# A graph layer's first stage: two node chunks beside each edge group, and an earlier release of a PSUM tile

## The reference, cut to what matters

```python
xn = layernorm(x)                                    # 20000 x 256
h = silu(edge_attr_8 @ fc_w1 / sqrt(8))              # radial network, first product
w = (h @ fc_w2 / sqrt(64)).reshape(-1, 5, 64)        # second product: five weights per channel
s, v = xn[:, :64][src], xn[:, 64:].reshape(-1, 64, 3)[src]
m0 = (w[:, 0] * s + w[:, 3] * dot(v, sh1) / sqrt(3)) / sqrt(2)
m1 = (w[:, 1] * s * sh1 + w[:, 2] * v + w[:, 4] * cross(v, sh1) / sqrt(2)) / sqrt(3)
x = x + xn + concat(segment_sum(m0, dst) @ lin_w0, segment_sum(m1, dst) @ lin_w1) / (16 * 8)
x = x + experts(layernorm(x))                        # later stages, not touched
```

## Time and profile before

| | us |
|---|---|
| median of three runs | 1472.23 |
| the profiled execution's own time | 1472.45 |
| its span, first to last instruction | 1470.6 |
| start of the next stage's loads (SP, line 354) | 386.23 |

### The profile page before, as it was taken

One profiled execution on the slowest core, in us unless ns is written; L12 is line 12 of the kernel. 1 busy time (PEld: TensorE's weight loads), 2 busy tenths in 40 slices (PEclk: granted clock), 3 DMA queues, 4 the chain that ended last, 5 costly groups with the idle time before them and its releaser, 6 DMA issues.

```text
span 1470.6 us, 26642 instructions
## 1 busy us (share of the span) xinstructions
PE 1217.7 (83%) x7872; PEld 1077.1 (73%) x7872; DVE 1007.6 (69%) x2132; ACT 930.6 (63%) x2048; POOL 1029.5 (70%) x975
## 2 busy tenths in 40 slices
PE   2335598898499433999999999999999999999993
PEld 0222365555355222999999999999999999999993
DVE  7889969997399795655756755755755575556653
ACT  4788967875266400666766766666766676657662
POOL 6886787875488402776777766777776777678785
PEclk9966788889799775999999999999999999999997
DMA  9999845543666302233433432243522343233333
GB/s 328 295 338 321 265 83 72 76 66 47 143 215 216 116 10 71 66 82 45 107 47 51 106 49 43 48 104 47 113 45 46 45 108 51 46 47 52 53 52 43
DMA packets 131626, 152.98 MB, mean 104 GB/s; under 512 B 17034, under 2 KB 118474, under 8 KB 131422
## 3 DMA queue, kind: packets, MB, share of 16 engines
q0 software_dynamic: 51456, 64.07, 27.0%
q1 hardware_dynamic: 58446, 66.59, 13.9%
q10 hardware_dynamic: 21648, 21.45, 4.2%
HBM read 98.79 MB, written 53.28 MB: 103 GB/s over the span
## 4 chain that ended last, share of the span: by engine, by line
PE 54%; issue 3%; POOL 2%; ACT 1%; DMA 1%; DVE 0%; ACTq 0%; POOLq 0%; DVEq 0%
PE f_ps_y L1523 26%; PE f_ps_h L1511 25%; PE f_ps_x L1501 2%; POOL out L1402 1%; POOL xg L1384 1%; POOL sg L1388 0%; DMA sg<-stat_rows,idx_row 0%; ACT y_all L1461 0%; ACT h_all L1451 0%; ACT h_hi L1450 0%; ACT f_xn L1435 0%; DMA out<-clean,put_now 0%; DMA sg<-stat_rows,idx_now 0%; DVE clean L1588 0%; DVE x_lo L1556 0%
## 5 line engine op out<-in xcount | busy, mean ns | idle before, releaser
L1450 ACT ACTIVATE h_hi<-f_ps_h,c_b 128x384 fp32r<-128x384 f32 (+1 forms) x416 | 236.8, 569 | 262.7 <-PE f_ps_h L1511 262.7
L1561 DVE TENSOR_TENSOR h_lo<-h_all,h_hi 128x768 fp32r<-128x768 f32 (+1 forms) x208 | 184.4, 887 | 256.9 <-ACT h_all L1451 256.3
L1523 PE MATMUL f_ps_y<-w_hi,h_hi 128*128 128x256 f32 x1136 | 325.4, 286 | 0.0
L1523 PE MATMUL f_ps_y<-w_lo,h_hi 128*128 128x256 f32 x1136 | 320.4, 282 | 0.0
L1523 PE MATMUL f_ps_y<-w_hi,h_lo 128*128 128x256 f32 x1136 | 320.2, 282 | 0.0
L1402 POOL DMA_INDIRECT out<-clean,put_now x159 | 262.0, 1648 | 56.7 <-issue 49.4
L1384 POOL DMA_INDIRECT xg<-out,idx_now x159 | 192.7, 1212 | 129.6 <-issue 119.4
L1511 PE MATMUL f_ps_h<-x_hi,w_hi 128*128 128x384 f32 (+1 forms) x832 | 272.3, 327 | 8.0 <-issue 3.5
L1511 PE MATMUL f_ps_h<-x_lo,w_hi 128*128 128x384 f32 (+1 forms) x832 | 269.8, 324 | 0.0
L1511 PE MATMUL f_ps_h<-x_hi,w_lo 128*128 128x384 f32 (+1 forms) x832 | 269.5, 324 | 0.0
L1451 ACT ACTIVATE h_all<-f_ps_h,c_b 128x384 f32<-128x384 f32 (+1 forms) x416 | 237.7, 571 | 0.0
(11 more groups left out here) (211 smaller groups left out, 2290.2 us busy)
## 6 DMA issues: line engine op xcount, KB each, us to landing
shared<-out SPq DMA_DIRECT2D x40, 512.0 KB, 4.0
w_raw<-in_w SPq DMA_DIRECT2D x16, 1024.0 KB, 5.4
xin<-in_x SPq DMA_DIRECT2D x24, 512.0 KB, 7.2
out<-xin ACTq DMA_DIRECT2D x24, 512.0 KB, 6.4
shared<-in_x SPq DMA_DIRECT2D x16, 512.0 KB, 6.7
out<-shared ACTq DMA_DIRECT2D x16, 512.0 KB, 6.1
dst_row<-in_dst SPq DMA_DIRECT2D x20, 256.0 KB, 3.9
xg<-out,idx_now POOLq DMA_INDIRECT x159
```

What stands on the lines that cost most here:

```text
L1450: nc.scalar.activation(h_hi[:, f, :n * P], ps_h[:, f % SLOTS, :n * P], ACT.Relu, bias=b1[:, e, f:f + 1])
L1523: ins = nc.tensor.matmul(ps_y[:, i], x[:, f, i * P:(i + 1) * P], weights[s][:, w], start=i != 1 and f == 0 and n == 0, stop=f == KF - 1 an ...
L1561: tt(h_lo[:, pair, :n * P], h_all[j % 2][:, :, :n * P], h_hi[:, pair, :n * P].bitcast(F32), ALU.subtract).then_inc(h_lo_ready, 1)
```

## The change

`STEPS` becomes 10. DVE takes two node chunks in each of steps 0 to 7, one of them inside `messages`. ACT adds two chunks for each group, in loops 1 to 9. The buffers of edge statistics go from four to eight (`AHEAD`), and DVE's statistics of edge groups run ahead: groups 3 to 9 in steps 0 to 3 (two a step), then group n in step n - 6, so that group 19 is done in step 13. POOL issues two gathers, one batch of node statistics and two of edge statistics in each round, and its last own node batch is number 6. Its gathers 14 to 19 now follow scatters 5, 6 and 7. The reciprocal square roots of edge groups 10 to 19 follow scatters 3 to 12. SP sends the embeddings and receivers of a group with each second chunk.

In `messages` the last reader of ps_w is brought forward by one instruction and raises a semaphore of its own, `w_taken`. PE's second product waits for that instead of `msg_ready`. PE's first product is issued before the aggregate. ACT copies the aggregate between the two halves of `rows_by_direction`, and the update behind the second.

```diff
@@ -136,13 +136,14 @@
     RING = 6
-    STEPS = 5
+    STEPS = 10
+    AHEAD = 8
     SLOTS = 14
...
     MAGIC = 0x5F3759DF
-    BY_POOL = 8
-    assert NC == 4 * STEPS
+    BY_POOL = 7
+    assert NC == 2 * STEPS
     with ExitStack() as ctx:
...
@@ -201,10 +202,10 @@
         edge_stats = [sb(f"edge_stats{h}", [P, GT, 6]) for h in range(2)]
-        edge_mv = [sb(f"edge_mv{h}", [P, GT, 2]) for h in range(4)]
+        edge_mv = [sb(f"edge_mv{h}", [P, GT, 2]) for h in range(AHEAD)]
         edge_var = sb("edge_var", [P, GT])
-        edge_rstd = [sb(f"edge_rstd{h}", [P, GT]) for h in range(4)]
-        edge_shift = [sb(f"edge_shift{h}", [P, GT]) for h in range(4)]
+        edge_rstd = [sb(f"edge_rstd{h}", [P, GT]) for h in range(AHEAD)]
+        edge_shift = [sb(f"edge_shift{h}", [P, GT]) for h in range(AHEAD)]
         y = [sb(f"y{h}", [P, GT, 4, D]) for h in range(2)]
...
@@ -262,6 +263,7 @@
         msg_ready = sem("msg_ready")
+        w_taken = sem("w_taken")
         row_ready = sem("row_ready")
...
@@ -320,31 +322,26 @@
             for c in range(NC):
-                for a in range(2):
-                    if 1 <= c and c + RING - 1 < NC:
+                if c:
+                    for a in range(2):
                         sp.wait_ge(x1_out[(c - 1) % RING][a], 16 * ((c - 1) // RING + 1))
-                        load_rows(c + RING - 1, a)
-                if 1 <= c and c + RING - 1 < NC:
+                        if c + RING - 1 < NC:
+                            load_rows(c + RING - 1, a)
                     sp.sem_inc(stored, 1)
...
                     sp.dma_start(chunks_needed[:], io["chunks"].rearrange("g o -> o g")).then_inc(chunks_known, 16)
-                if c % 4 == 1:
-                    next_embedding(c // 4)
-                    if c > 4:
-                        next_receivers(c // 4 - 1)
-            for c in range(NC - RING, NC):
-                for a in range(2):
-                    sp.wait_ge(x1_out[c % RING][a], 16 * (c // RING + 1))
-                sp.sem_inc(stored, 1)
-                if c == NC - RING + 1:
-                    next_receivers(STEPS - 1)
-                if c == NC - RING + 3:
-                    next_embedding(STEPS)
-            next_receivers(STEPS)
-            for g in range(STEPS + 1, EG):
+                if c % 2:
+                    next_embedding(c // 2)
+                    if c > 2:
+                        next_receivers(c // 2 - 1)
+            for a in range(2):
+                sp.wait_ge(x1_out[(NC - 1) % RING][a], 16 * ((NC - 1) // RING + 1))
+            sp.sem_inc(stored, 1)
+            next_receivers(STEPS - 1)
+            for g in range(STEPS, EG):
                 next_embedding(g)
...
@@ -370,12 +367,12 @@
             def edge_scales(g):
-                h = g % 4
+                h = g % AHEAD
                 pool.wait_ge(edge_mv_ready, g + 1)
...
                     pool.wait_ge(edge_rstd_ready, g)
-                if g >= 4:
-                    pool.wait_ge(y_first, g - 3)
+                if g >= AHEAD:
+                    pool.wait_ge(y_first, g - AHEAD + 1)
                 chain.link(nc.gpsimd.tensor_scalar(edge_var[:], edge_mv[h][:, :, 1], EPS, None, ALU.add))
...
@@ -422,20 +419,21 @@
             for n in range(3, BY_POOL):
+                gather(2 * n - 1)
+                gather(2 * n)
                 node_scales(n)
-                for g in (2 * n - 1, 2 * n):
-                    if g < SLOTS:
-                        gather(g)
-                if n % 2:
-                    edge_scales(n // 2 + 2)
+                edge_scales(2 * n - 3)
+                if 2 * n - 2 < STEPS:
+                    edge_scales(2 * n - 2)
+            gather(2 * BY_POOL - 1)
             pool.wait_ge(chunks_known, 16)
...
                 scatter(g)
-                if STEPS <= g + 4 < EG - 1:
-                    edge_scales(g + 5)
-                if 1 <= g < 4:
-                    gather(SLOTS + 2 * g - 2)
-                    gather(SLOTS + 2 * g - 1)
+                if STEPS <= g + 7 < EG:
+                    edge_scales(g + 7)
+                if 5 <= g < 8:
+                    gather(SLOTS + 2 * (g - 5))
+                    gather(SLOTS + 2 * (g - 5) + 1)
             pool.wait_ge(scattered, 64 * (EG + 1))
@@ -454,8 +452,8 @@
                     ins = nc.scalar.activation(y[g % 2][:, t, 0, :], rows[g][:, t, :], ACT.Identity,
-                                               bias=edge_shift[g % 4][:, t:t + 1],
-                                               scale=edge_rstd[g % 4][:, t:t + 1])
+                                               bias=edge_shift[g % AHEAD][:, t:t + 1],
+                                               scale=edge_rstd[g % AHEAD][:, t:t + 1])
                 ins.then_inc(y_first, 1)
@@ -510,31 +508,30 @@
             rows_by_direction(0, (2, 3))
-            add_own_rows(2)
             radial_hidden(1)
...
             rows_by_direction(1, range(GT))
-            add_own_rows(3)
             for g in range(1, STEPS):
-                c = 4 * g
-                add_own_rows(c)
+                add_own_rows(2 * g)
+                radial_hidden(g + 1)
+                if g + 1 == STEPS:
+                    add_own_rows(2 * g + 1)
+                    store_rows(NC - 1, 1)
+                next_rows(g + 1)
+                rows_by_direction(g + 1, (0, 1))
                 take_agg(g - 1)
-                radial_hidden(g + 1)
-                next_rows(g + 1)
-                add_own_rows(c + 1)
-                rows_by_direction(g + 1, (0, 1))
+                if g + 1 < STEPS:
+                    add_own_rows(2 * g + 1)
+                rows_by_direction(g + 1, (2, 3))
                 take_upd(g - 1)
-                add_own_rows(c + 2)
-                rows_by_direction(g + 1, (2, 3))
-                add_own_rows(c + 3)
-            store_rows(NC - 1, 1)
             for g in range(STEPS, EG + 1):
                 if g + 1 < EG:
+                    radial_hidden(g + 1)
                     next_rows(g + 1)
-                    rows_by_direction(g + 1, range(GT))
+                    rows_by_direction(g + 1, (0, 1))
                 take_agg(g - 1)
                 if g + 1 < EG:
-                    radial_hidden(g + 1)
+                    rows_by_direction(g + 1, (2, 3))
                 take_upd(g - 1)
@@ -548,7 +545,7 @@
                 if g:
-                    pe.wait_ge(msg_ready, g)
+                    pe.wait_ge(w_taken, g)
                 for t in range(GT):
...
@@ -583,9 +580,9 @@
                     radial_second(g + 1)
-                aggregate(g)
                 if g + 2 < EG:
                     radial_first(g + 2)
+                aggregate(g)
                 transform(g)
@@ -655,10 +652,10 @@
                 chain.link(ins)
-                if g >= 4:
-                    v.wait_ge(coef_ready, g - 3)
+                if g >= AHEAD:
+                    v.wait_ge(coef_ready, g - AHEAD + 1)
                 for t in range(GT):
-                    ins = nc.vector.bn_aggr(edge_mv[g % 4][:, t], edge_stats[g % 2][:, t])
+                    ins = nc.vector.bn_aggr(edge_mv[g % AHEAD][:, t], edge_stats[g % 2][:, t])
                 ins.then_inc(edge_mv_ready, 1)
@@ -708,31 +705,39 @@
                 chain.mark(tt(tmp_d[:], tmp_f[:], w(3), ALU.mult))
+                chain.wait(1)
+                tt(vec(tmp_h), vec(tmp_a), w3(4), ALU.mult).then_inc(w_taken, 1)
                 chain.mark(tt(tmp_g[:], tmp_b[:], tmp_c[:], ALU.add))
-                chain.wait(2)
-                chain.mark(tt(vec(tmp_h), vec(tmp_a), w3(4), ALU.mult))
-                chain.wait(2)
+                chain.wait(1)
                 chain.mark(tt(msg[h][:, :, :, 0], tmp_e[:], tmp_d[:], ALU.add))
+                v.wait_ge(w_taken, g + 1)
                 chain.wait(1)
...
                 receivers(g)
-                if g + 1 < STEPS:
-                    node_coefs(BATCH[4 * g + 2])
-                    node_statistics(4 * g + 4)
-                    messages(g, 4 * g + 5)
-                    edge_statistics(g + 3)
-                    node_coefs(BATCH[4 * g + 4])
-                    edge_coefs(g + 2)
-                    node_statistics(4 * g + 6)
-                    node_statistics(4 * g + 7)
+                if g + 2 < STEPS:
+                    messages(g, 2 * g + 4)
+                    node_coefs(BATCH[2 * g + 2])
+                    node_statistics(2 * g + 5)
                 else:
-                    if g + 1 == STEPS:
+                    if g + 2 == STEPS:
                         node_coefs(BATCH[NC - 1])
                     messages(g)
-                    edge_statistics(g + 3)
-                    edge_coefs(g + 2)
+                for n in range(EG):
+                    if statistics_step(n) == g:
+                        edge_statistics(n)
+                for n in range(EG):
+                    if coefs_step(n) == g:
+                        edge_coefs(n)
+
```

(7 more changed lines are left out.)

## The result

The changed kernel takes 1483.63 us (median of 11 runs, 1476.69 to 1489.16) against 1472.19 us for the kernel before beside it (11 runs). The ratio is 1.0072, 95% interval 1.0055 to 1.0089: slower by 0.7%. The profiled execution took 1486.09 us with a span of 1484.3 us. It lies 2.5 us above the median, so its trace overstates the loss a little.

The account below looks back on a forecast made before the run. POOL's serial chain of scatters, each waiting for landings, was taken as the bound. Scatter 0 at 124.7 plus 50, 11.05, 66, 121.6 and 9.28 gave stage end 382.6, 3.6 us earlier: 1468.8 us, range 1459 to 1478.

Parts of the forecast that it names:

- The slower rival: Landing waits of scatters 0 to 4: five intervals at 14.70 us, 12.4 us more, stage end 395.0, 1481 us; chance 0.16.
- 11.05: POOL's uncrowded scatter interval in us, from scatters 4 to 14 of before; used for scatters 4 to 5 and 8 to 19.
- I take 12.5, a little under the middle: Scatters 0 to 4 on POOL: four intervals of 12.5 us, between 11.05 and 14.70, 50 us in all.
- where the rival turns the sign: Early scatter interval from which the slower rival puts the stage end again at 386.2: 13.4 us.
- The price of 14.70: Distance in us between scatters 0 and 1 before the change, beside node loads; upper bound for the early intervals.
- the 3.0 us of ACT's lateness: Scatters 4 to 19 of before: 168.75 us against 165.75, so ACT's lateness cost the tail 3.0 us.
- a denser DVE: DVE busier beside POOL's scatter issues, stretching its descriptors: under 2 us more for all scatters.
- the shared port: Port from which DVE locks GpSimd out during some DVE instructions, so a denser DVE would stretch POOL's descriptors.
- a sign of being wrong: POOL's timeline: the prediction is wrong if a scatter from 5 on waits for ACT's copy.
- POOL's rounds of 17 us: POOL before scatter 0: eight gathers, a node batch and two edge groups' square roots, 16.95 us a round.
- The third rival: All of DVE's removed waiting comes through: stage end 353, 33 us less, 1439 us; chance 0.03.
- DVE's wait for ps_w: DVE waiting for PE's second product: 17.4 us in nine waits before, claimed to go to nothing.

Follow-up runs that it names:

- four profiles with the changed order: One profile each of the changed kernel, e6, e10 and e11, sharing its order of scatters and loads; stage ends 396.9, 394.8, 388.8 and 400.2 us.
- e8: Changed kernel with SP loading one tile of four in each half of chunks 8 to 19; 1470.2 us, not the same work, only the first stage is read.
- e1: Kernel before with only the early release of ps_w and PE's first product ahead of the aggregate; 1538.11 us against 1536.59, ratio 1.0019.
- e12: Kernel before with only the early ps_w release and PE's new order, repeated on another chip; 1472.92 us against 1472.8, ratio 1.0004.
- e11: Changed kernel with 48 increments of an unused semaphore at the start of SP's program; 1489.86 us, stage end 400.2.
- e6: Changed kernel in which PE's second product waits for the whole of the messages again, PE's new order kept; 1484.12 us in one run.
- e5: Changed kernel with PE's old order (aggregate, then the next first product), ps_w still released early; 1544.88 us in one run, before 1472.82.
- e3: Changed kernel in which POOL starts scatter 0 only after all 20 chunks are stored and gathers 14 to 19 issued; 1631.94 us in one run.
- e10: Changed kernel with 16 increments of an unused semaphore at the start of SP's program; 1477.19 us, stage end 388.8.

## Why the prediction was wrong

Direction and size were wrong, and the bound was right. The slower rival ("the crowd costs its full price", 1481 us, stage end 395.0) named the place and the mechanism, the landings of scatters 0 to 4. That its stage end fits the mean of 395.2 is half luck: it put all of its 12.4 us into five intervals of 14.7, and they were 13.5 and brought 6.3. The terms, against the means of the four profiles with the changed order:

| term | predicted | changed kernel | mean of four |
|---|---|---|---|
| scatter 0 at | 124.7 | 125.4 | 127.0 |
| scatters 0 to 5 | 50 + 11.05 | 68.0 | 67.3 |
| scatters 5 to 8 | 66 | 68.2 | 67.4 |
| scatters 8 to 19 | 121.6 | 125.9 | 124.1 |
| last scatter | 9.3 | 9.5 | 9.4 |
| stage end | 382.6 | 396.9 | 395.2 |

**The step that failed** is "I take 12.5, a little under the middle, since chunks now move at 2 in 18.4 to 20.8 us". Measured are 13.5 us over five intervals, not 12.5 over four and then 11.05. That is 6.3 of the 12.6 us by which the stage end was missed, 4.7 of them in the four intervals and 1.6 in the fifth. The first two intervals have the price of before's crowded one or more, 14 to 16, and with a lower rate of chunks it did not fall; e8 shows that it is the transfers' price, and by its 57.8 us how little is left without a part of them. The crowd also lasted past the 175 us where I let it end: the fourth and fifth intervals were still 12.5 and 12.1. My own sum had DVE at the chunks until 195.9 (its last chunk was done at 195.5), and ACT's last node store went out at 218.3. I also counted wrongly where the rival turns the sign: with five intervals instead of four it is from 12.9 us each, not 13.4.

This step alone would have given 1468.8 + 6.3 = 1475.1, within my range. The rest is in small terms that all went one way: by the means of the table 2.3 us at scatter 0, 1.4 at scatters 5 to 8, 2.5 behind scatter 8, and 2.45 on the way into the next stage.

The price of 14.70 was taken from an interval whose row names ACT's copy, not a landing. The trace of before bears the reading out all the same. The last DMA of scatter 0, issued at 129.71, landed 7.9 us later, at 137.6, and ACT's copy ended at 138.2, so both were over just before scatter 1 at 138.49.

**Smaller misses.** The intervals behind scatter 8 cost 11.3 instead of 11.05. They did so before the change too: scatters 8 to 19 took 124.5 us there, 122.7 in e1 and 127.1 in e12, against 124.1 now. So 11.05, from one stretch of one trace, was too low, and the 3.0 us of ACT's lateness did not come back. For a denser DVE I had allowed under 2 us in all, from issue rows of 1.62 and 1.55 us, though DVE was still at work beside the first of the two at 1.55 (343.76). Single intervals reach further, as one of e11 in POOL's timeline, where four issues that take 6.2 us in the quiet take 9.4:

```profile
285.38 1.62 POOL L402 DMA_INDIRECT out<-rows,upd_row  x1 [1.64 <-ACT rows L498]
287.31 1.58 POOL L402 DMA_INDIRECT out<-rows,upd_row  x1 [0.31 <-issue]
289.19 2.38 POOL L402 DMA_INDIRECT out<-rows,upd_row  x1 [0.30 <-issue]
291.88 3.83 POOL L402 DMA_INDIRECT out<-rows,upd_row  x1 [0.30 <-issue]
...
299.94 2.73 POOL L402 DMA_INDIRECT out<-rows,upd_row  x1 [2.82 <-DMA out<-rows,upd_row]
```

No run tried what stretches them, so the shared port that the prediction names remains an argument. The first row is also a scatter that waited for ACT's copy, 1.64 us, which the prediction had named as a sign of being wrong. Scatter 0 was 2.3 later in the mean, and the way into the next stage took 2.45 us more, which nothing in the trace of before announced.

**Right.** The chain on POOL ends the stage of the changed kernel; that DVE ended earlier does not show in it; node batches, gathers and POOL's rounds of 17 us came as counted; in the changed kernel no scatter behind the fifth waited for ACT. The third rival (all of DVE's waiting comes through, 1439) is ruled out: DVE ended 13.7 us earlier and the stage 10.7 later.

**Wrong without harm.** DVE's wait for ps_w did not go to nothing. PE's timeline of the changed kernel has the reason: the second product stands behind the transform in PE's queue, and that waits for ACT's copy of the aggregate, which in ACT's loop comes behind the next group's y and half of its products.

```profile
224.68 2.72 PE L569 MATMUL ps_agg<-lin,agg 128*128 128x128 f32 x16 [4.11 <-ACT agg L490]
227.33 4.63 PE L550 MATMUL ps_w<-fc,hidden 64*128 64x320 f32 x8
...
242.36 2.05 PE L569 MATMUL ps_agg<-lin,agg 128*128 128x128 f32 x16 [1.16 <-ACT agg L490]
244.34 2.42 PE L550 MATMUL ps_w<-fc,hidden 64*128 64x320 f32 x8
```

The transform starts when ACT has copied, in brackets, and the second product right behind it, in 4.63 us or 2.42 (the granted clock in this stretch is 0.82 in the mean). An earlier semaphore on ps_w moves nothing there; that fits the equal waits of e6 (14.4) and of the changed kernel (16.9). The last message came at 349 instead of 328 to 336, still 38 us ahead of scatter 19.

## What to carry to other kernels

When a stage is ended by a serial chain of transfers, look first at what runs beside each link of it: making the engines' work even can spread bulk transfers over the chain's first links, and each then pays for them. Price a crowded link by the crowded row that the trace has, and not below it, until a run shows that less crowd is cheaper. Take the price of a free link from more than one trace where there are 11 of them in the sum. Before moving a copy or a product inside one engine's loop, follow the cycle through all queues; here one swap on PE (e5) was worth 60 us only because another engine's order had changed.

## What the runs showed of the hardware

- From one scatter of 4 x 128 rows of 1 KB with addition to the next, which waits for its landing, it takes 10.2 us in the quiet (e3), 11.05 to 11.8 in the mean with the engines at work, and 11.5 to 16 beside bulk loads and stores, where the window from 123 to 164 us has a DMA share of 0.96 to 1.00 (the four kernels of the changed order). Its DMAs landed 3.7 to 3.9 us after issue in the quiet tail, and 5.2 to 7.4 us after issue beside those transfers (medians of the first five scatters in e6 and e10).
- The stage end varies by over 10 us between four kernels that differ in nothing that was found to matter (388.8 to 400.2, one profile each). In its whole time the changed kernel spreads over 12.5 us in 11 runs, the one before over 5.1.
- One of the two chips that the experiments used took 64 us more for the whole (before: 1536.6 against 1472.8), while the first stage ended at 382.0 in e1, as elsewhere. Why is open.
